# Graph attention: the masks of two chunks packed as the two bytes of one 16-bit number, and turned by one set of transposes

## The chip, the cores and the metric

One core of one Trainium2 chip. The metric is the device time of one execution in microseconds, as the median of several runs. The engines are TensorE (PE; PEld for its weight loads), VectorE (DVE), ScalarE (ACT), GpSimd (POOL) and SyncE (SP, which only issues transfers here). Each works through its own list of instructions in order, and they wait for one another by semaphores.

## The reference

For each of 8 graphs with 2048 nodes and 256 features (`x` is 8 x 2048 x 256 fp32, `adj` 8 x 2048 x 2048 int32, about one entry in 512 set):

```python
h  = relu(layernorm(x))
Wh = h @ W
f1, f2 = Wh @ a[:256], Wh @ a[256:]
e  = leaky_relu(f1[:, None] + f2[None, :], 0.2)
p  = softmax(where(adj > 0, e, -9e15), axis=0)   # over i: each column j sums to one
out = x + elu(p @ Wh)
```

The softmax runs down the columns of `adj`. The kernel therefore keeps column j on a partition and the 2048 rows i along the free dimension, and needs the mask in that turned layout.

## The kernel before, in words

A batch is one graph. Its 2048 columns are taken as 16 chunks of 128 (128 chunks in all, CH). The main loop has a step s per chunk; every engine runs the same list of steps, written out in its own order, and works on chunks at different distances from s.

- **Masks.** GpSimd issues `load_raw(pair)` (L880 to L883) every second step: 1 MB of `adj`, 2048 rows by 256 columns, turned from int32 into bf16 by the transfer, into one of two buffers `raw`. VectorE makes one mask per step, `make_mask(s + 2)` (L762): 0 where there is an edge and -2^56 where there is none, as bf16, from one half of the columns. TensorE turns it in 16 transposes of 128 x 128 bf16 into `tp`, two banks of PSUM (L434 to L440), one chunk per step: `transpose_mask(s + 1)`, after the block of stored products and before the transposes of x.
- **Scores.** VectorE adds the turned mask to `f1_row` (f1 of all rows i, on every partition) and takes the maximum in the same instruction, into `prob` (L773). TensorE may turn the next mask only when these scores are read (`wait(pe, scores, c)`), as there is one `tp`.
- **Softmax.** ScalarE adds f2, applies the leaky ReLU (L590), negates the maximum (L592) and takes the exponential with its sum (L598). GpSimd makes the inverse of the sum (L890, L893) and the high fp16 half of the first 1024 probabilities (`direct`, L896); ScalarE makes the high half of the other 1024 (`stored`, L604); VectorE makes both low halves (L787, L792).
- **Products.** TensorE multiplies the direct halves with Wh in the next step (L504, L506, L511: 24 matmuls), and one row block of the stored halves of eight chunks (L486 to L488: 24 matmuls). Finished row blocks are scaled, given the ELU and added to x (L620 to L651, L806, L812, L916).
- **Projections, 17 chunks ahead.** x comes in chunks of 128 rows (`load_x`, L346), VectorE takes the statistics (L737, L742), GpSimd normalises (L910), TensorE transposes and multiplies with W (L429, L417). f1 is written to memory and read back onto all partitions (`f1_row`). For the last quarter of a batch that is a round trip just before the next batch's first scores.

The order of VectorE in a step is: scores(s), statistics, mask(s + 2), low half of Wh(s + 17), low halves of chunk s - 1, then what finishes a row block. The order of GpSimd is: inverse and product of chunk s - 1, normalise, an addition by transfer (L916), the load of a mask pair.

The lines that the change turns on:

```python
nc.vector.tensor_scalar(neg[:, c % 2], raw[:, pair % 2, :, c % 2 * P:(c % 2 + 1) * P], 0.0, -NOT_AN_EDGE, ALU.is_le, ALU.mult)
...
for m in range(C):
    last = nc.tensor.transpose(tp_b[:, m * P:(m + 1) * P], neg[:, c % 2, m, :], ident_b[:])
```

Of the kernel before, what the change touches and what calls it, by code (L numbers as in the profile page):

```python
# [6 lines left out]
ALU = mybir.AluOpType  # L7
# [2 lines left out]
F32 = mybir.dt.float32  # L10
F16 = mybir.dt.float16
BF16 = mybir.dt.bfloat16

P = 128
ALPHA = 0.2
EPS = 1e-5
NOT_AN_EDGE = 2.0 ** 56
P_BITS = 14
W_TOP = 16.0


def graph_attention(nc, x, adj, W, a, out):

    B, N, F = x.shape
# [23 lines left out]
    with ExitStack() as ctx:  # L50
# [6 lines left out]
        def sem(name):  # L57
            return ctx.enter_context(nc.semaphore(name))

        raw = sb("raw", [P, 2, C, 2 * P], BF16)  # L60
        neg = sb("neg", [P, 2, C, P], BF16)
        f1_row = sb("f1_row", [P, 2, N], F32)
        prob = sb("prob", [P, 2, N + 2], F32)
        direct = sb("direct", [P, 2, 2, HALF], F16)
# [38 lines left out]
        tp = psum("tp", [P, 2, 512], F32)  # L103
        pre = psum("pre", [P, 512], F32)
        tp_b = tp[:].rearrange("p h c -> p (h c)").bitcast(BF16)
        acc_banks = acc[:].rearrange("p (h m) o -> p h (m o)", m=2)

        raw_in = [sem(f"raw_in{i}") for i in range(2)]
        x_in_s = [sem(f"x_in_s{i}") for i in range(RX)]
        x_early_in = [sem(f"x_early_in{i}") for i in range(4 + EARLY // 4 - 1)]  # L110
        x_res_in = [sem(f"x_res_in{i}") for i in range(RY)]
# [206 lines left out]
        def rows_of(tensor, k):  # L318
            b, i = finishing[k]
            if single(k):  # L320
                r = (2 * NB - 2 + (i == 8)) * P
                return tensor[b, r:r + P, :].rearrange("(t p) f -> p t f", p=P)
            r = (NB + 2 * i if i < 4 else 2 * (i - 4)) * P
            return tensor[b, r:r + 2 * P, :].rearrange("(t p) f -> p t f", p=P)

        def h_prime(k):
            b, i = finishing[k]
# [8 lines left out]
        def y_buf(k):  # L336
            return y[:, k % RY, 0:width(k) // FO, :]

        finish_index = {item: k for k, item in enumerate(finishing)}

        block = ctx.enter_context(nc.Block())

        @block.sync
        def _(sp):
            def load_x(c):
                if c - RX >= EARLY:  # L346
                    sp.wait_ge(xn_ready, c - RX + 1)
                sp.dma_start(x_buf(c), x[c // C, c % C * P:(c % C + 1) * P, :]).then_inc(x_in_s[(c - EARLY) % RX], 16)

            def write_f1(piece):  # L350
                index = pieces_sent(piece)
                sp.wait_ge(f1_turned, index + 1)
                b, q = divmod(piece, 4)
                rows = f1_dram[b, 512 * q:512 * (q + 1)].rearrange("(c g r) -> g c r", g=4, r=32)
                for g in range(4):
                    sp.dma_start(rows[g], f1_t[32 * g:32 * g + 4, index % 2, :]).then_inc(f1_written[index % 2], 16)

            def read_f1(piece):
                index = pieces_sent(piece)
                b, q = divmod(piece, 4)  # L360
                sp.wait_ge(f1_written[index % 2], 64 * (index // 2 + 1))
                wait(sp, scores, C * (b - 1))
                sp.dma_start(f1_row[:, b % 2, 512 * q:512 * (q + 1)],
                             f1_dram[b:b + 1, 512 * q:512 * (q + 1)].to_broadcast([P, 512])
                             ).then_inc(f1_row_in[b % 2], 16)

            def load_y(step):
                for k in finish(step):
                    wait(sp, y_out[k % RY], 16 * (k // RY))
                    sp.dma_start(y_buf(k), rows_of(x, k)).then_inc(x_res_in[k % RY], 16)  # L370

            def send_y(step):
                for k in finish(step):
                    wait_for_y(sp, k)
                    sp.dma_start(rows_of(out, k), y_buf(k)).then_inc(y_out[k % RY], 16)

            for c in range(4):
                sp.dma_start(x_buf(c), x[0, c * P:(c + 1) * P, :]).then_inc(x_early_in[c], 16)
                if c == 0:
                    sp.dma_start(w_raw, W.rearrange("(k p) o -> p k o", p=P)).then_inc(w_in, 16)  # L380
                    sp.dma_start(a_one, a.rearrange("o one -> one o")).then_inc(a_in, 16)
            for g in range(1, EARLY // 4):
                r = 4 * g % C * P
                sp.dma_start(x_early[:, 4 * g:4 * g + 4, :],
                             x[4 * g // C, r:r + 4 * P, :].rearrange("(c p) f -> p c f", p=P)
                             ).then_inc(x_early_in[3 + g], 16)
            for c in range(EARLY, EARLY + RX):
                load_x(c)
            for s in range(FIRST, END + 2):
                if chunk(s + 24) and s + 24 >= EARLY + RX:  # L390
                    load_x(s + 24)
                if chunk(s + LEAD - 1) and (s + LEAD - 1) % 4 == 3 and read_alone((s + LEAD - 1) // 4):
                    read_f1((s + LEAD - 1) // 4)
                if s <= CH + 2:
                    load_y(s + 1)
                    send_y(s - 2)
                else:
                    send_y(s - 1)
                    load_y(s + 1)
                if chunk(s + LEAD) and (s + LEAD) % 4 == 3 and sent((s + LEAD) // 4):  # L400
                    write_f1((s + LEAD) // 4)
                    if (s + LEAD) // 4 % 4 > 0:
                        read_f1((s + LEAD) // 4 - 1)
            for i in range(RY):
                sp.wait_ge(y_out[i], 16 * len([k for k in range(len(finishing)) if k % RY == i]))

        @block.tensor
        def _(pe):
# [21 lines left out]
                                               ident[:])  # L430
                last.then_inc(xt_ready, 1)

            def transpose_mask(c):
                pe.wait_ge(neg_ready, c + 1)  # L434
                if c == 0:
                    pe.wait_ge(ident_ready, 1)
                wait(pe, scores, c)
                for m in range(C):
                    last = nc.tensor.transpose(tp_b[:, m * P:(m + 1) * P], neg[:, c % 2, m, :], ident_b[:])  # L439
                last.then_inc(tp_ready, 1)  # L440

            def warm_up(count):
# [98 lines left out]
            for s in range(-18, 0):  # L541
                if s == -1:
                    spread_last_f1()
                    transpose_mask(0)
                transpose_x(s + LEAD + 1)
                if chunk(s + LEAD):
                    make_wh(s + LEAD)
            for s in range(END + 2):
# [4 lines left out]
                    extra_blocks(s - 2)  # L553
                if n is not None:
                    store_block(n)
                if chunk(s + 1):
                    transpose_mask(s + 1)
                if chunk(s + LEAD + 1):
                    transpose_x(s + LEAD + 1)
                if chunk(s - 1):  # L560
# [131 lines left out]
        def _(dve):  # L692
# [12 lines left out]
            def multiply_w(i):  # L705
                k, side = divmod(i, 2)
                dve.wait_ge(a_spread, 1)
                nc.vector.tensor_tensor_reduce(
                    out=w_a[:, i, :], in0=w_raw[:, k, :], in1=a_row[:, side, :], scale=1.0, scalar=0.0,
                    op0=ALU.mult, op1=ALU.add, accum_out=w_cat[:, k, FO + side:FO + side + 1]).then_inc(w_ready, 1)  # L710

            def largest_of_all():
# [42 lines left out]
                nc.vector.scalar_tensor_tensor(out=offset[:, rs], in0=mv[:, rs, 0], scalar=-1.0, in1=rstd[:, rs],  # L755
                                               op0=ALU.mult, op1=ALU.mult).then_inc(offset_s, 1)

            def make_mask(c):
                pair = c // 2
                dve.wait_ge(raw_in[pair % 2], 16 * (pair // 2 + 1))  # L760
                wait(dve, tp_ready, c - 1)
                nc.vector.tensor_scalar(neg[:, c % 2], raw[:, pair % 2, :, c % 2 * P:(c % 2 + 1) * P], 0.0, -NOT_AN_EDGE, ALU.is_le, ALU.mult  # L762
                                        ).then_inc(neg_ready, 1)

            def mask_scores(c):
                b, j = divmod(c, C)
                dve.wait_ge(tp_ready, c + 1)
                if j == 0:
                    dve.wait_ge(f1_row_in[b % 2], 64 * (b // 2 + 1) - (16 if b % 2 == 0 else 0))
                if c == 0:  # L770
                    dve.wait_ge(f1_last, 1)
                wait(dve, lo_stored, c - 1)
                nc.vector.tensor_tensor_reduce(  # L773
                    out=prob[:, c % 2, 0:N], in0=tp_b, in1=f1_row[:, b % 2, :], scale=1.0, scalar=-3.0e38,
                    op0=ALU.add, op1=ALU.max, accum_out=prob[:, c % 2, N:N + 1]).then_inc(scores, 1)

            def split_v_low(c):
                dve.wait_ge(v_hi, c + 1)
# [41 lines left out]
            for s in range(FIRST, END + 2):  # L820
# [20 lines left out]
                    multiply_w(3)  # L841
                if offset_at(s) is not None and s >= 0:
                    make_offset(offset_at(s))
                if chunk(s + 2) and s >= 0:
                    make_mask(s + 2)
                if s == 0:
                    split_v_low(LEAD - 1)
                if chunk(s + LEAD) and s != -1:
# [2 lines left out]
                    turn_f1((s + LEAD) // 4)  # L851
                if chunk(s - 1):
                    split_low(s - 1)
                if s == -5:
                    make_mask(0)
                if s == -4:
                    make_mask(1)
                for k in finish(s - 1 if s <= CH + 1 else s):
                    finish_elu(k)
                n = block_at(s)  # L860
# [4 lines left out]
        def _(pool):  # L865
# [10 lines left out]
            pool.wait_ge(const_ready, 1)  # L876


            def load_raw(pair):
                wait(pool, neg_ready, 2 * pair - 2)  # L880
                b, q = divmod(pair, C // 2)
                nc.gpsimd.dma_start(raw[:, pair % 2], adj[b].rearrange("(c p) j -> p c j", p=P)[  # L882
                    :, :, 2 * P * q:2 * P * (q + 1)]).then_inc(raw_in[pair % 2], 16)  # L883

            def split_high(c):
                p = prob[:, c % 2, :]
# [32 lines left out]
            for s in range(FIRST, END + 2):  # L919
# [4 lines left out]
                for k in finish(s - 2):  # L924
                    if k < summed_by_dma:
                        finish_add(k)
                if s % 2 == 0 and s >= 0 and chunk(s + 4):
                    load_raw(s // 2 + 2)
                if s == -22:
                    normalise(0)  # L930
                if 0 < s + LEAD + 2 and s < 0:
                    normalise(s + LEAD + 2)
                if s == -16:
                    load_raw(0)
                if s == -12:
                    load_raw(1)
                if s == -24:
                    root(0)
                if s == -21:
# [21 lines left out]
```

## Time and profile before

| | us |
|---|---|
| median of 3 runs | 992.19 (990.35 to 992.49) |
| the profiled execution | 987.88 |
| its span | 986.1 |
| PE busy | 950.0 |
| DVE busy | 920.7 |
| ACT busy | 879.3 |
| POOL busy | 645.3 |

The span runs from the first to the last instruction of the profiled execution; its time has 1.8 us more around it. Busy times are unions over the span and include time in which an instruction has started but is held up. Matmuls overlap in the pipeline, so the mean duration of one (0.27 us) is longer than the distance to the next (0.11 us).

### The profile page before, as it was taken

How to read it: one execution, taken by the hardware profiler on the slowest of the kernel's cores; microseconds unless marked ns; L12 is line 12 of the kernel's file. 1: busy time of each engine (PE TensorE's matmuls, PEld its weight loads, DVE VectorE, ACT ScalarE, POOL GpSimd, SP SyncE). 2: the span in 40 equal slices, each digit the busy share in tenths (PEclk: the TensorE clock that was granted, in tenths of full speed). 3: DMA queues.
4: the chain of work that ended last, by engine and by line, in shares of the span. 5: the costliest groups of instructions: out<-in, count | busy, mean ns of one | idle time of the engine just before them, and what ended most of it. 6: DMA issues, size and time to landing. Idle time of an engine off the chain costs nothing.

```text
span 986.1 us, 23861 instructions
## 1 busy us (share of the span) xinstructions
PE 950.0 (96%) x8993; PEld 840.0 (85%) x8993; DVE 920.7 (93%) x1271; ACT 879.3 (89%) x1237; POOL 645.3 (65%) x676
## 2 busy tenths in 40 slices
PE   8878999999999999999999999999999999999996
PEld 6666888889888898888888888888988989898896
DVE  8799989999899998999989998999999999999975
ACT  4788989999999999999999899999999999898985
POOL 6567665776766776876767776677676775555540
PEclk8899999999999999999999999999999999999898
DMA  9477667889879889799979988979987978979724
GB/s 233 83 107 108 97 108 122 147 162 156 149 136 176 146 155 167 119 180 149 161 147 144 173 148 151 154 141 172 156 163 123 172 133 138 170 113 158 143 65 140
DMA packets 199093, 142.13 MB, mean 144 GB/s; under 512 B 7361, under 2 KB 187841, under 8 KB 198978
## 3 DMA queue, kind: packets, MB, share of 16 engines
q0 software_dynamic: 140160, 81.80, 61.5%
q1 hardware_dynamic: 58818, 58.81, 20.8%
q8 instruction: 72, 1.18, 0.5%
q14 instruction: 43, 0.35, 0.1%
HBM read 176.16 MB, written 16.84 MB: 196 GB/s over the span
## 4 chain that ended last, share of the span: by engine, by line
POOL 32%; PE 30%; issue 25%; DVE 5%; DMA 4%; ACT 2%; POOLq 0%; SPq 0%; DVEq 0%; ACTq 0%
POOL direct L896 10%; POOL xn L910 6%; POOL raw L882 5%; POOL inv L893 4%; PE acc L511 4%; PE acc L504 4%; PE acc L506 4%; PE tp L439 3%; PE acc_st L486 3%; PE acc_st L487 3%; PE acc_st L488 3%; POOL y L916 3%; PE pre L417 3%; POOL rstd L904 2%; POOL small_total L890 2%
## 5 line engine op out<-in xcount | busy, mean ns | idle before, releaser
L773 DVE CUSTOM_DVE_ANT_0 prob<-tp,f_row 128x2048 f32<-128x2048 bf16 x128 | 292.0, 2282 | 21.5 <-DMA f_row<-f_scratch 14.9
L590 ACT ACTIVATE prob<-prob,f 128x2049 f32<-128x2049 f32 x128 | 257.6, 2013 | 5.4 <-DVE prob L773 5.4
L486 PE MATMUL acc_st<-v,stored 128*128 128x256 f16 x960 | 261.5, 272 | 0.8 <-ACT part L620 0.8
L488 PE MATMUL acc_st<-v,stored 128*128 128x256 f16 x960 | 261.7, 273 | 0.0
L487 PE MATMUL acc_st<-v,stored 128*128 128x256 f16 x960 | 261.6, 273 | 0.0
L598 ACT ACTIVATE prob<-prob,shift 128x2048 f32<-128x2048 f32 x128 | 256.5, 2004 | 4.0
L896 POOL TENSOR_TENSOR direct<-prob,inv 128x1024 f16<-128x1024 f32 x128 | 243.5, 1902 | 10.0
L504 PE MATMUL acc<-v,direct 128*128 128x256 f16 x1024 | 233.4, 275 | 5.4 <-ACT z_direct L626 3.5
L506 PE MATMUL acc<-v,direct 128*128 128x256 f16 x1024 | 233.3, 274 | 0.0
L890 POOL TENSOR_SCALAR small_total<-total 128x1 f32<-128x1 f32 x128 | 29.8, 233 | 272.8 <-ACT prob L598 271.4
L604 ACT ACTIVATE stored<-prob,inv 128x1024 f16<-128x1024 f32 x128 | 146.1, 1142 | 47.6 <-POOL inv L893 47.6
L787 DVE SCALAR_TENSOR_TENSOR direct<-prob,inv,direct 128x1024 f16<-128x1024 f32 x128 | 162.0, 1266 | 12.2 <-POOL direct L896 12.1
L792 DVE SCALAR_TENSOR_TENSOR stored<-prob,inv,stored 128x1024 f16<-128x1024 f32 x128 | 163.7, 1279 | 0.1
L439 PE MATMUL tp<-ident_b,neg 128*128 128x128 bf16 x2048 | 136.1, 220 | 6.1 <-DVE prob L773 6.1
L439 PEld LDWEIGHTS tp<-ident_b,neg 128*128 128x128 bf16 x2048 | 125.4, 98 | 12.1 <-issue 9.2
L511 PE MATMUL acc<-v,direct 128*128 128x256 f16 x1024 | 133.6, 274 | 0.0
L762 DVE TENSOR_SCALAR neg<-raw 128x2048 bf16<-128x2048 bf16 x128 | 129.9, 1015 | 0.8 <-DMA raw<-in_adj 0.8
L417 PE MATMUL pre<-w_cat,h_t 128*128 128x258 f32 x444 | 117.8, 388 | 4.6 <-ACT h_t L610 4.1
L504 PEld LDWEIGHTS acc<-v,direct 128*128 128x128 f16 x1024 | 100.9, 99 | 17.7 <-ACT z_direct L626 4.9
L487 PEld LDWEIGHTS acc_st<-v,stored 128*128 128x128 f16 x960 | 93.7, 98 | 22.0
L506 PEld LDWEIGHTS acc<-v,direct 128*128 128x128 f16 x1024 | 100.9, 99 | 12.0
L910 POOL TENSOR_SCALAR xn<-x_in,rstd,offset 128x256 f32<-128x256 f32 x108 | 107.3, 994 | 5.4 <-DVE offset L755 3.0
(94 smaller groups left out, 1383.9 us busy)
## 6 DMA issues: line engine op xcount, KB each, us to landing
raw<-in_adj POOLq DMA_DIRECT2D x64, 1024.0 KB, 11.2
y<-in_x SPq DMA_DIRECT2D x63, 256.0 KB, 3.1
out<-y SPq DMA_DIRECT2D x63, 256.0 KB, 2.2
y<-elu POOLq DMA_DIRECT2D x56, 256.0 KB, 5.0
x_in<-in_x SPq DMA_DIRECT2D x108, 128.0 KB, 3.3
f_row<-f_scratch SPq DMA_DIRECT2D x31, 256.0 KB, 6.5
stored<-in_x SPq DMA_DIRECT2D x4, 512.0 KB, 6.9
f_scratch<-f_t SPq DMA_DIRECT2D x124, 0.5 KB
```

Of the source, the lines that this page charges most:

```text
L439: last = nc.tensor.transpose(tp_b[:, m * P:(m + 1) * P], neg[:, c % 2, m, :], ident_b[:])
L486: nc.tensor.matmul(bank[:, 0:FO], p_st[:, 0, rows], v_c[:, 0, :], start=(c == 0), stop=False)
L487: nc.tensor.matmul(bank[:, 0:FO], p_st[:, 0, rows], v_c[:, 1, :], start=False, stop=False)
L488: last = nc.tensor.matmul(bank[:, 0:FO], p_st[:, 1, rows], v_c[:, 0, :], start=False, stop=(c == G - 1))
L504: nc.tensor.matmul(acc[:, m, :], p_d[:, 0, rows], v_c[:, 0, :], start=(j == 0 and m % 2 == 0), stop=False, skip_group_check=True)
L506: nc.tensor.matmul(acc[:, m, :], p_d[:, 0, rows], v_c[:, 1, :], start=False, stop=False, skip_group_check=True)
L511: last = nc.tensor.matmul(acc[:, m, :], p_d[:, 1, rows], v_c[:, 0, :], start=False, stop=(j == C - 1), skip_group_check=True)
L590: nc.scalar.activation(p_top, p_top, ACT.Prelu, bias=f2, alpha=ALPHA).then_inc(leaky, 1)
L598: nc.scalar.activation(p, p, ACT.Exp, bias=shift[:, c % R:c % R + 1], accum_out=total[:, c % R:c % R + 1]).then_inc(prob_ready, 1)
L773: nc.vector.tensor_tensor_reduce(out=prob[:, c % 2, 0:N], in0=tp_b, in1=f1_row[:, b % 2, :], scale=1.0, scalar=-3.0e38, op0=ALU.add, op1=A ...
L896: nc.gpsimd.tensor_tensor(direct[:, c % 2, 0, :], p[:, 0:HALF], k.to_broadcast([P, HALF]), ALU.mult).then_inc(hi_direct, 1)
L910: nc.gpsimd.tensor_scalar(xn_buf(c), x_buf(c), rstd[:, c % RS:c % RS + 1], offset[:, c % RS:c % RS + 1], ALU.mult, ALU.add).then_inc(xn_re ...
```

## The change

The mask becomes one byte: 0 for an edge, 192 for none. Columns 2k and 2k + 1 of a 256-column stretch of `adj` go to two different chunks (even columns to the one, odd ones to the other), so that the bytes of neighbouring columns form one 16-bit number. 16 transposes of these numbers, as bf16, turn both chunks at once, every second step; the scores instruction reads every second byte of `tp`. It subtracts f1, scaled by 2^-48 in advance, from the byte and multiplies by -2^48, which gives f1 where there is an edge and f1 - 192 x 2^48 elsewhere.

As chunks are now alternate columns, rows of x, of the output and the order of i follow: chunk 2q + t holds rows 256q + 2p + t. A mask instruction takes the even or the odd rows i of a 256-column stretch and makes half of both chunks' masks; it still has 2048 elements. The loads are halved in size and doubled in number (four buffers of half the size). Masks are made one step earlier (s + 3 in place of s + 2), and a pair's transposes come on odd steps.

```diff
 BF16 = mybir.dt.bfloat16
+U8 = mybir.dt.uint8
 P = 128
...
 EPS = 1e-5
-NOT_AN_EDGE = 2.0 ** 56
+F1_SCALE = 2.0 ** -48
+NOT_AN_EDGE = 192.0
 P_BITS = 14
...
             return ctx.enter_context(nc.semaphore(name))
-        raw = sb("raw", [P, 2, C, 2 * P], BF16)
+        raw = sb("raw", [P, 4, G, 2 * P], BF16)
         neg = sb("neg", [P, 2, C, P], BF16)
+        neg_bytes = neg[:].rearrange("p b m j -> p b (m j)").bitcast(U8).rearrange("p b (t q j) -> p b t q j", t=2, q=G)
         f1_row = sb("f1_row", [P, 2, N], F32)
...
         tp_b = tp[:].rearrange("p h c -> p (h c)").bitcast(BF16)
+        tp_bytes = tp[:].rearrange("p h c -> p (h c)").bitcast(U8).rearrange("p (i t) -> p t i", t=2)
         acc_banks = acc[:].rearrange("p (h m) o -> p h (m o)", m=2)
-        raw_in = [sem(f"raw_in{i}") for i in range(2)]
+        raw_in = [sem(f"raw_in{i}") for i in range(4)]
         x_in_s = [sem(f"x_in_s{i}") for i in range(RX)]
...
             if single(k):
-                r = (2 * NB - 2 + (i == 8)) * P
-                return tensor[b, r:r + P, :].rearrange("(t p) f -> p t f", p=P)
+                r = (2 * NB - 2) * P
+                return tensor[b, r:r + 2 * P, :].rearrange("(p t) f -> p t f", p=P)[:, (i == 8):(i == 8) + 1, :]
             r = (NB + 2 * i if i < 4 else 2 * (i - 4)) * P
-            return tensor[b, r:r + 2 * P, :].rearrange("(t p) f -> p t f", p=P)
+            return tensor[b, r:r + 2 * P, :].rearrange("(p t) f -> p t f", p=P)
         def h_prime(k):
...
             return y[:, k % RY, 0:width(k) // FO, :]
+        def x_rows(c):
+            b, j = divmod(c, C)
+            q, t = divmod(j, 2)
+            return x[b, 2 * P * q:2 * P * (q + 1), :].rearrange("(p t) f -> t p f", t=2)[t]
+        def masks_at(s):
+            if s < 0:
+                return [s + 5] if s >= -5 and s < -3 else []
+            return [2, 3] if s == 0 else ([s + 3] if s + 3 < CH else [])
         finish_index = {item: k for k, item in enumerate(finishing)}
...
                     sp.wait_ge(xn_ready, c - RX + 1)
-                sp.dma_start(x_buf(c), x[c // C, c % C * P:(c % C + 1) * P, :]).then_inc(x_in_s[(c - EARLY) % RX], 16)
+                sp.dma_start(x_buf(c), x_rows(c)).then_inc(x_in_s[(c - EARLY) % RX], 16)
             def write_f1(piece):
...
             for c in range(4):
-                sp.dma_start(x_buf(c), x[0, c * P:(c + 1) * P, :]).then_inc(x_early_in[c], 16)
+                sp.dma_start(x_buf(c), x_rows(c)).then_inc(x_early_in[c], 16)
                 if c == 0:
...
                 r = 4 * g % C * P
-                sp.dma_start(x_early[:, 4 * g:4 * g + 4, :],
-                             x[4 * g // C, r:r + 4 * P, :].rearrange("(c p) f -> p c f", p=P)
+                sp.dma_start(x_early[:, 4 * g:4 * g + 4, :].rearrange("p (q t) f -> p q (t f)", t=2),
+                             x[4 * g // C, r:r + 4 * P, :].rearrange("(q p t) f -> p q (t f)", p=P, t=2)
                              ).then_inc(x_early_in[3 + g], 16)
...
                 last.then_inc(xt_ready, 1)
-            def transpose_mask(c):
-                pe.wait_ge(neg_ready, c + 1)
-                if c == 0:
+            def transpose_masks(pair):
+                pe.wait_ge(neg_ready, 2 * pair + 2)
+                if pair == 0:
                     pe.wait_ge(ident_ready, 1)
-                wait(pe, scores, c)
+                wait(pe, scores, 2 * pair)
                 for m in range(C):
-                    last = nc.tensor.transpose(tp_b[:, m * P:(m + 1) * P], neg[:, c % 2, m, :], ident_b[:])
+                    last = nc.tensor.transpose(tp_b[:, m * P:(m + 1) * P], neg[:, pair % 2, m % 2 * G + m // 2, :],
+                                               ident_b[:])
                 last.then_inc(tp_ready, 1)
...
                     spread_last_f1()
-                    transpose_mask(0)
+                    transpose_masks(0)
                 transpose_x(s + LEAD + 1)
...
                     store_block(n)
-                if chunk(s + 1):
-                    transpose_mask(s + 1)
+                if chunk(s + 1) and s % 2 == 1:
+                    transpose_masks((s + 1) // 2)
                 if chunk(s + LEAD + 1):
...
                 nc.vector.tensor_tensor_reduce(
-                    out=w_a[:, i, :], in0=w_raw[:, k, :], in1=a_row[:, side, :], scale=1.0, scalar=0.0,
+                    out=w_a[:, i, :], in0=w_raw[:, k, :], in1=a_row[:, side, :], scale=(F1_SCALE, 1.0)[side], scalar=0.0,
                     op0=ALU.mult, op1=ALU.add, accum_out=w_cat[:, k, FO + side:FO + side + 1]).then_inc(w_ready, 1)
...
                                                op0=ALU.mult, op1=ALU.mult).then_inc(offset_s, 1)
-            def make_mask(c):
-                pair = c // 2
-                dve.wait_ge(raw_in[pair % 2], 16 * (pair // 2 + 1))
-                wait(dve, tp_ready, c - 1)
-                nc.vector.tensor_scalar(neg[:, c % 2], raw[:, pair % 2, :, c % 2 * P:(c % 2 + 1) * P], 0.0, -NOT_AN_EDGE, ALU.is_le, ALU.mult
-                                        ).then_inc(neg_ready, 1)
+            def make_masks(n):
+                pair, t = divmod(n, 2)
+                dve.wait_ge(raw_in[n % 4], 16 * (n // 4 + 1))
+                wait(dve, tp_ready, pair - 1)
+                nc.vector.tensor_scalar(neg_bytes[:, pair % 2, t], raw[:, n % 4], 0.0, NOT_AN_EDGE,
+                                        ALU.is_le, ALU.mult).then_inc(neg_ready, 1)
             def mask_scores(c):
                 b, j = divmod(c, C)
-                dve.wait_ge(tp_ready, c + 1)
+                dve.wait_ge(tp_ready, c // 2 + 1)
                 if j == 0:
...
                 nc.vector.tensor_tensor_reduce(
-                    out=prob[:, c % 2, 0:N], in0=tp_b, in1=f1_row[:, b % 2, :], scale=1.0, scalar=-3.0e38,
-                    op0=ALU.add, op1=ALU.max, accum_out=prob[:, c % 2, N:N + 1]).then_inc(scores, 1)
+                    out=prob[:, c % 2, 0:N], in0=tp_bytes[:, c % 2, :], in1=f1_row[:, b % 2, :], scale=-1.0 / F1_SCALE,
+                    scalar=-3.0e38, op0=ALU.subtract, op1=ALU.max, accum_out=prob[:, c % 2, N:N + 1]).then_inc(scores, 1)
             def split_v_low(c):
...
                     make_offset(offset_at(s))
-                if chunk(s + 2) and s >= 0:
-                    make_mask(s + 2)
+                for n in masks_at(s):
+                    make_masks(n)
                 if s == 0:
...
                     split_low(s - 1)
-                if s == -5:
-                    make_mask(0)
-                if s == -4:
-                    make_mask(1)
                 for k in finish(s - 1 if s <= CH + 1 else s):
...
             pool.wait_ge(const_ready, 1)
-            def load_raw(pair):
-                wait(pool, neg_ready, 2 * pair - 2)
+            def load_raw(n):
+                pair, t = divmod(n, 2)
+                wait(pool, neg_ready, n - 3)
                 b, q = divmod(pair, C // 2)
-                nc.gpsimd.dma_start(raw[:, pair % 2], adj[b].rearrange("(c p) j -> p c j", p=P)[
-                    :, :, 2 * P * q:2 * P * (q + 1)]).then_inc(raw_in[pair % 2], 16)
+                nc.gpsimd.dma_start(raw[:, n % 4], adj[b].rearrange("(q p t) j -> t p q j", p=P, t=2)[
+                    t, :, :, 2 * P * q:2 * P * (q + 1)]).then_inc(raw_in[n % 4], 16)
             def split_high(c):
...
                         finish_add(k)
-                if s % 2 == 0 and s >= 0 and chunk(s + 4):
-                    load_raw(s // 2 + 2)
+                if s >= -1 and chunk(s + 5):
+                    load_raw(s + 5)
                 if s == -22:
...
                     normalise(s + LEAD + 2)
-                if s == -16:
-                    load_raw(0)
-                if s == -12:
-                    load_raw(1)
+                if s in (-16, -15, -12, -11):
+                    load_raw((-16, -15, -12, -11).index(s))
                 if s == -24:
```

## Rows read from the trace of the kernel before

**Rows 1.** Page, part 1: busy us (share of the span) x instructions of each engine.

```profile
span 986.1 us, 23861 instructions
PE 950.0 (96%) x8993; PEld 840.0 (85%) x8993; DVE 920.7 (93%) x1271; ACT 879.3 (89%) x1237; POOL 645.3 (65%) x676
```

**Rows 2.** Windows, by batch: us of each engine (x instructions), clock, DMA, GB/s.

```profile
core 0: us, PE busy (x) PEld busy (x) DVE busy (x) ACT busy (x) POOL busy (x), PEclk, DMA share, GB/s
32.10:144.60 112.50, 97.85 (x884) 82.75 (x883) 105.30 (x140) 98.17 (x138) 74.71 (x76) 0.97 0.68 102
144.60:730.30 585.70, 580.88 (x5597) 517.93 (x5596) 563.05 (x780) 544.32 (x769) 410.32 (x419) 1.00 0.88 152
730.30:846.00 115.70, 115.41 (x1121) 103.23 (x1120) 112.16 (x140) 108.15 (x151) 78.73 (x81) 1.00 0.87 148
846.00:949.00 103.00, 97.53 (x982) 86.86 (x980) 95.62 (x92) 92.44 (x98) 56.11 (x59) 0.97 0.77 129
949.00:986.10 37.10, 29.61 (x272) 26.30 (x269) 20.64 (x30) 21.22 (x32) 5.37 (x6) 0.93 0.38 122
```

**Rows 3.** Chain of waits, 400 to 420 us: start, us, engine, tile, line.

```profile
by line: PE pre L417 13.1%; PE acc_st L487 13.1%; PE acc_st L486 13.1%; PE acc L511 13.1%; PE acc_st L488 13.1%; PE acc L506 12.0%; PE acc L504 11.4%; PE tp L439 8.9%; PE pre L429 2.3%
...
405.55 0.89 PE tp L439 x16
...
412.79 0.89 PE tp L439 x16
```

**Rows 4.** Waits, 144.6 to 730.3 us: total us, times, longest.

```profile
POOL small_total L890 <- ACT prob L598: 155.6, 71, 4.6
ACT stored L604 <- POOL inv L893: 24.8, 41, 1.0
DVE prob L773 <- DMA f_row<-f_scratch: 13.7, 6, 3.0
ACT f L579 <- PE pre L417: 6.0, 24, 0.4
ACT prob L590 <- DVE prob L773: 4.1, 5, 1.4
```

**Rows 5.** Source view, VectorE lines: count, ns min/median/max, first and last start.

```profile
L762 DVE TENSOR_SCALAR neg<-raw x128: 675/715/2374, 27.3 to 938.3; 128x2048 bf16<-128x2048 bf16 x128
L773 DVE CUSTOM_DVE_ANT_0 prob<-tp,f_row x128: 2269/2278/2293, 32.1 to 949.0; 128x2048 f32<-128x2048 bf16 x128
L792 DVE SCALAR_TENSOR_TENSOR stored<-prob,inv,stored x128: 1270/1273/1419, 43.5 to 960.4; 128x1024 f16<-128x1024 f32 x128
```

**Rows 6.** Windows, by batch, of the mask instruction's line alone.

```profile
32.10:144.60 112.50, 15.37 (x16) 0.97 0.68 102
144.60:730.30 585.70, 74.70 (x80) 1.00 0.88 152
730.30:846.00 115.70, 19.69 (x16) 1.00 0.87 148
846.00:949.00 103.00, 18.51 (x14) 0.97 0.77 129
```

**Rows 7.** Timeline of VectorE, 424 to 426 us: start, us, line, tiles.

```profile
424.69 0.18 DVE L742 BATCH_NORM_AGGREGATE mv<-stats 128x2 f32<-128x6 f32 x1
424.79 0.89 DVE L762 TENSOR_SCALAR neg<-raw 128x2048 bf16<-128x2048 bf16 x1
425.61 0.41 DVE L779 TENSOR_TENSOR v<-pre,v 128x256 f16<-128x256 f32 x1
```

**Rows 8.** Timeline of GpSimd, 422 to 427 us.

```profile
423.25 1.90 POOL L896 TENSOR_TENSOR direct<-prob,inv 128x1024 f16<-128x1024 f32 x1
425.13 0.99 POOL L910 TENSOR_SCALAR xn<-x_in,rstd,offset 128x256 f32<-128x256 f32 x1
```

**Rows 9.** Page, part 6 (DMA issues), and the costliest lines: GpSimd's issues.

```profile
raw<-in_adj POOLq DMA_DIRECT2D x64, 1024.0 KB, 11.2
x_in<-in_x SPq DMA_DIRECT2D x108, 128.0 KB, 3.3
...
L882 POOL DMA_DIRECT2D raw<-in_adj x64 | 83.5, 1305 | 0.0
L916 POOL DMA_DIRECT2D y<-elu x56 | 52.1, 930 | 0.0
```

## The prediction

> **What bounds the kernel now.** I read the page's busy shares first [rows 1]: TensorE, VectorE and ScalarE are all near or above 90% busy, so no single share names the bound, and the next view has to be taken by stage. There are 128 chunks in eight batches of 16. Batches 1 to 5 are alike and take 585.7 us together (117.1 each), with TensorE busy for 580.9, VectorE for 563.1 and ScalarE for 544.3 [rows 2]. Batches 0, 6 and 7 have lighter VectorE work or an interrupted TensorE; 37 us of tail follow, and 32 us of head stand before.
>
> TensorE really is full. The chain of waits over one stretch of batch 3 is TensorE alone, and two successive bursts of mask transposes start 7.24 us apart, each 0.89 us long [rows 3]. So 16 transposes cost 0.89 us of a step, and 12% of TensorE's step is the thing that the change halves. But the other engines stand right behind it. VectorE lacks only 585.7 - 563.1 = 22.6 us over five batches, and 13.7 us of that are waits for f1's row at the batch edges [rows 4], which no faster TensorE shortens. ScalarE's 544.3 us become 579.2 with what it waits for the inverse (24.8), for TensorE's projections (6.0) and for scores (4.1) [rows 4]; the inverse is a reply that its own loop needs. So a shorter TensorE step uncovers engines that are only a few per cent shorter, and any VectorE time that the change adds is uncovered almost at once.
>
> **The change part by part.**
>
> *Transposes.* Sixteen per two chunks in place of 32: 64 bursts of 0.89 us less, 57 us of TensorE. In steps 1 to 126 the remaining bursts fall on odd steps, where they wait for the odd chunk's scores as each burst waits for its predecessor's now; the even chunk's scores come a step later, and the odd chunk's need no new transpose. Nothing is delayed by that.
>
> *The mask instruction.* Still one per chunk, still 2048 elements, but it writes bytes in place of 16-bit numbers. This is the term that decides. Its row now is 675 ns at least and 715 in the median [rows 5]. The score instruction on the same engine, with the same 2048 elements and two operands, takes 2278 ns [rows 5]. If both have the same fixed part, then one unit of work q solves a + q = 675 and a + 4q = 2278: q is 534 ns and a is 141 ns, so the mask runs four elements in the time in which the scores run one. No row shows a one-operand VectorE instruction of this size with a byte result. The two ends are therefore +0 (it stays at 675) and +1.60 us (it falls to 2278). The mask differs from every slow row in two ways, one tensor operand and 16-bit numbers on both sides, and the change takes the second away and leaves the first. I take the step between, two elements at a time: a + 2q = 1.21 us, +0.534 us per mask, which in ratio is also about as far from the one row as from the other. Both ends stay in the range or the rivals.
>
> The Trainium skill speaks to this place, and against the change: "DVE: opcode table, instruction layouts, handler registers and perf-mode slots", section 7, says that the engine's four-per-cycle mode is chosen only where source and destination are both 2 bytes wide, and that a one-source operation with a stream of another width is left with the one- and the two-per-cycle modes. "VectorE: DVE Perf Modes", in its tier table, gives 693 ns for 2048 bf16 elements and 1227 ns for 2048 fp32 elements of a one-source operation. The trace's 675 to 715 ns agree with the first; no run here shows the second, by which the term would be +0.53 us, as in the sum.
>
> *Its stalls.* The mask's mean is far above its minimum: 74.7 us for 80 masks, 20.7 more than 80 x 0.675 [rows 6]. What it waits for is GpSimd: a mask that starts at 424.79, while the product of 423.25 to 425.15 runs, takes 0.89 us, that is 0.36 until the product ends and then about the 0.53 of its pure work; the GpSimd instruction behind it (xn at 425.13) is stretched in its turn [rows 7, 8]. If VectorE becomes the slow engine, the product of the chunk before is ready earlier within VectorE's step, so I keep a quarter of these stalls (5 us over five batches) and both ends, 0 and 20.7.
>
> *Scores.* Same instruction and element count; its mask operand is read as every second byte of PSUM in place of every 16-bit number, with another constant. No row shows such a read. It writes one fp32 per 1.04 ns already, so I take no change; were it half as fast it would cost 2 us a step, and that is in the slow rival.
>
> *Loads of the mask.* 128 of half the size in place of 64. One issue holds GpSimd for 1.31 us now, and that of a 256 KB transfer for 0.93 [rows 9], so a half-size issue lies between 0.65 (half) and 1.31; at 1.1 GpSimd's 410.3 us over five batches become about 446 of 585.7 [rows 2]. What hides it is GpSimd's wait for the exponential, 155.6 us there [rows 4]. The lead is two steps, some 14.5 us, as before, against 11.2 us to landing for 1 MB now [rows 9]; without that cover the mask would wait for the load. Rows of x, of the residual and of the output are taken in pairs of the same 1 KB runs or longer ones; 3.3 us to landing for an x chunk [rows 9] has many steps of lead: nothing.
>
> **The sum.** Batches 1 to 5: VectorE without its stalls 563.1 - 20.7 = 542.4; 80 longer masks +42.7; the idle time of now, 22.6, which is mostly the batch edge's f1 row; a quarter of the stalls, 5. That is 612.7 against 585.7: +27.0. Batch 0 [rows 2, 6]: 105.3 - 4.6 + 8.5 = 109.2 on VectorE in 112.5; its 7.2 us of idle take up most of it: +2. Batch 6: 112.2 - 8.9 + 8.5 = 111.8, with 3.5 idle and 1 of stalls 116.3 against 115.7: +0.6. Batch 7 (14 masks): 95.6 - 9.1 + 7.5 = 94.0, with its 7.4 idle and 1 of stalls 102.4 against 103.0, and TensorE is freed: -1. Head: two masks before the first scores, +1. Tail: 0. In all +29.6. The profiled execution took 987.9 us (span 986.1 and 1.8 around it), so it would take 1017.5; the median of the runs lies 4.3 higher, which gives 1021.8. I put the forecast at 1019.
>
> The likeliest case's own range: down to 995 if all stalls vanish, half the idle time goes too, and batch 7 gains most of TensorE's 6 us; up to 1046 if all stalls stay and batch 0 pays in full.
>
> **Rivals.**
>
> *The mask keeps its rate* (or most of it), and the change is faster. Then TensorE's step falls to 6.8 us, and VectorE and ScalarE decide. ScalarE needs 579 us of 586 with its waits, so batches 1 to 5 gain 0 to 20 us; I take 10, with 2 in batch 6 and 3 in batch 7: 15 us, about 975. For it: 57 us of the fullest engine go, and nothing in the trace shows a byte result. Against it: the quick rate is seen only with 16-bit numbers on both sides.
>
> *The longer mask is swallowed.* VectorE's 20.7 us of stalls and 22.6 of idle over five batches (43.3) happen to equal the added 42.7. If all of it gives way, the batches stay at 117 us: 988 to 994, no change. Against it: the f1 row's wait is a round trip through memory at the batch edge that a longer mask doesn't shorten.
>
> *One element at a time.* The byte result (or the byte read in the scores) brings VectorE to the rate of the scores row: +1.60 us per mask. Batches 1 to 5: 542.4 + 128.2 + 22.6 + 5 = 698.2, +112; batch 0 +18, batch 6 +17, batch 7 +10, head +3: +160, about 1150. This decides from any price above the 0.28 us per mask that 22.6 us of VectorE idle over 80 masks can hide. For it: the other large VectorE rows run so, as the 1024 elements of the low half in 1273 ns [rows 5]. Against it: the mask keeps its single operand in SBUF.
>
> The side on which it ends hangs on the same point in all of them: below about 0.28 us per mask the saved transposes win or nothing is seen; above it VectorE sets a longer step.
>
> **Chances.** Half rate with VectorE as the bound 0.68; mask at its rate 0.15; swallowed 0.05; one at a time 0.12. A change of under 0.2% can't be told from none here. Faster: the second case and a little of the first's lower end, 0.16. Same: the swallowed case and a little beside it, 0.06. Slower: 0.78. The range, 976 to 1046, holds the likeliest case, the swallowed one and half of the faster one; it leaves out the one-at-a-time case and the other half of the faster, 0.2 together.
>
> **What would show it.** The mask's minimum should read 1.2 us (675 and 2278 are the rivals'), the scores 2.28. TensorE's bursts of mask transposes should be half as many, and TensorE should show gaps before the transposes or the direct products, its share falling to about 88% (893 of 1016 us). VectorE should have next to no idle in mid-batch, with steps of 7.6 us. GpSimd's wait for the exponential should stay above 1 us a step and no mask should wait for its load. The forecast is wrong if VectorE shows idle in mid-batch, if a mask waits for a transfer, or if a batch in the middle takes less than 117 us.

## The result, and the profile after

The changed kernel takes 1006.57 us (median of 4 runs, 1005.56 to 1007.15) against 992.34: ratio 1.0144, 95% interval 1.0125 to 1.0163. It is 14 us slower; the forecast was 1019. The profiled execution took 1005.56 us, 17.7 more than that of before (987.88, which lies further below its median).

The busy shares and the windows by batch of the changed kernel, with the columns of [rows 1] and [rows 2] (same batches, read at its own first scores):

```profile
span 1003.7 us, 21811 instructions
PE 918.0 (91%) x7969; PEld 782.7 (78%) x7969; DVE 960.0 (96%) x1271; ACT 879.8 (88%) x1237; POOL 752.7 (75%) x740
```

```profile
33.60:151.30 117.70, 96.67 (x751) 79.33 (x750) 113.13 (x141) 98.26 (x137) 84.88 (x82) 0.88 0.69 98
151.30:745.40 594.10, 558.86 (x4965) 482.02 (x4963) 585.61 (x779) 543.76 (x770) 482.00 (x461) 1.00 0.90 150
745.40:863.30 117.90, 110.69 (x989) 95.37 (x987) 116.80 (x140) 107.76 (x151) 91.29 (x87) 1.00 0.88 144
863.30:967.40 104.10, 92.10 (x863) 77.12 (x862) 99.24 (x90) 93.47 (x99) 65.57 (x65) 1.00 0.79 127
967.40:1003.70 36.30, 28.85 (x262) 25.16 (x259) 20.66 (x30) 21.29 (x32) 5.36 (x6) 0.96 0.36 125
```

VectorE is busy for 585.6 of the 594.1 us of batches 1 to 5; TensorE has dropped behind it. The chain of waits in mid-kernel (420 to 450 us), all TensorE before [rows 3], is now VectorE and pieces without a named wait ("issue"):

```profile
by line: issue 33.4%; DVE prob L792 23.4%; DVE stored L811 15.9%; DVE direct L806 15.8%; DVE v L798 5.5%; DVE z_st L825 5.1%; DVE stats L756 4.7%; DVE mv L761 1.0%; DVE neg L781 0.9%; DVEq L821 0.7%; DVEq L246 0.5%; DVE elu L831 0.4%; DVE f
```

The mask and scores of the changed kernel (source view, ns min/median/max, to be read against [rows 5]), and the mask's windows in batches 1 to 5 (against [rows 6]):

```profile
L781 DVE TENSOR_SCALAR neg<-raw x128: 1208/1224/2668, 27.8 to 950.5; 128x2048 uint8<-128x2048 bf16 x128
L792 DVE CUSTOM_DVE_ANT_0 prob<-tp,f_row x128: 2272/2280/2294, 33.6 to 967.4; 128x2048 f32<-128x2048 uint8 x128
```

```profile
151.30:745.40 594.10, 107.92 (x80) 1.00 0.90 150
```

The mask went from 675 to 1208 ns at least; the scores read every second byte at no price. VectorE's waits in batches 1 to 5 were 13.7 us for f1's row [rows 4]; now they are

```profile
DVE prob L792 <- DMA f_row<-f_scratch: 2.1, 3, 1.2
DVE prob L792 <- DVE stored L811: 0.3, 2, 0.2
```

### The profile page after: what moved, and what is told of

It is laid out like the page before. It is cut to its first block, busy times and chain, and to the rows that moved or that the text cites. A ratio compares the mean times of both kernels' runs of the same rounds, so it can differ in the third digit from the quotient of the medians.

```text
span 1003.7 us, 21811 instructions
## 1 busy us (share of the span) xinstructions
PE 918.0 (91%) x7969; PEld 782.7 (78%) x7969; DVE 960.0 (96%) x1271; ACT 879.8 (88%) x1237; POOL 752.7 (75%) x740
## 4 chain that ended last, share of the span: by engine, by line
DVE 46%; issue 32%; POOL 10%; DMA 5%; PE 4%; ACT 2%; DVEq 1%; SPq 1%; POOLq 0%; ACTq 0%
DVE stored L811 11%; DVE direct L806 11%; DVE prob L792 10%; DVE v L798 4%; POOL direct L912 4%; DVE stats L756 3%; DVE neg L781 3%; DMA f_row<-f_scratch 2%; DMA f_scratch<-f_t 2%; POOL raw L898 2%; DVE z_st L825 1%; POOL inv L909 1%; POOL y L932 1%; DVE elu L831 1%; DVE mv L761 1%
## 5 line engine op out<-in xcount | busy, mean ns | idle before, releaser
L792 DVE CUSTOM_DVE_ANT_0 prob<-tp,f_row 128x2048 f32<-128x2048 uint8 x128 | 292.2, 2283 | 10.0 <-DMA f_row<-f_scratch 4.4
L523 PE MATMUL acc<-v,direct 128*128 128x256 f16 x1024 | 236.9, 277 | 8.7 <-ACT z_direct L645 5.0
L525 PE MATMUL acc<-v,direct 128*128 128x256 f16 x1024 | 236.6, 277 | 0.0
L781 DVE TENSOR_SCALAR neg<-raw 128x2048 uint8<-128x2048 bf16 x128 | 182.0, 1423 | 0.0
L906 POOL TENSOR_SCALAR small_total<-total 128x1 f32<-128x1 f32 x128 | 41.1, 321 | 179.8 <-ACT prob L617 136.3
L898 POOL DMA_DIRECT2D raw<-in_adj x128 | 156.3, 1221 | 0.2 <-POOL xn L926 0.2
L530 PE MATMUL acc<-v,direct 128*128 128x256 f16 x1024 | 134.5, 275 | 1.6 <-DVE direct L806 1.6
L926 POOL TENSOR_SCALAR xn<-x_in,rstd,offset 128x256 f32<-128x256 f32 x108 | 123.1, 1140 | 12.2 <-DVE offset L774 12.1
L523 PEld LDWEIGHTS acc<-v,direct 128*128 128x128 f16 x1024 | 101.9, 100 | 23.2 <-ACT z_direct L645 7.0
L530 PEld LDWEIGHTS acc<-v,direct 128*128 128x128 f16 x1024 | 100.4, 99 | 15.8 <-DVE direct L806 3.5
L525 PEld LDWEIGHTS acc<-v,direct 128*128 128x128 f16 x1024 | 101.7, 99 | 13.0
```

The source lines that it names most:

```text
L523: nc.tensor.matmul(acc[:, m, :], p_d[:, 0, rows], v_c[:, 0, :], start=(j == 0 and m % 2 == 0), stop=False, skip_group_check=True)
L525: nc.tensor.matmul(acc[:, m, :], p_d[:, 0, rows], v_c[:, 1, :], start=False, stop=False, skip_group_check=True)
L530: last = nc.tensor.matmul(acc[:, m, :], p_d[:, 1, rows], v_c[:, 0, :], start=False, stop=(j == C - 1), skip_group_check=True)
L792: nc.vector.tensor_tensor_reduce(out=prob[:, c % 2, 0:N], in0=tp_bytes[:, c % 2, :], in1=f1_row[:, b % 2, :], scale=-1.0 / F1_SCALE, scala ...
```

## The experiments

Theory A: the byte result halves the mask's rate, VectorE becomes the bound, and the halved transposes are worth nothing at that price. The rivals: the doubled loads on GpSimd (B), TensorE still sharing the bound (C). Ratios are against the kernel before.

**The mask at its old rate (e1).** The changed kernel with 16-bit results (not the masks of the graph):

```diff
-                nc.vector.tensor_scalar(neg_bytes[:, pair % 2, t], raw[:, n % 4], 0.0, NOT_AN_EDGE,
-                                        ALU.is_le, ALU.mult).then_inc(neg_ready, 1)
+                out16 = neg[:, pair % 2].rearrange("p (q t) j -> p q (t j)", t=2) if t else raw[:, n % 4]
+                nc.vector.tensor_scalar(out16, raw[:, n % 4], 0.0, -6.0234375, ALU.is_le, ALU.mult).then_inc(neg_ready, 1)
```

> The changed kernel, but each mask instruction writes 2048 16-bit numbers (the even one over its own input, the odd one over both halves of the mask buffer), so the masks are not those of the graph; transposes, loads and waits stay. Theory A (the loss is VectorE's time for the byte result): the mask is back at 0.68 us at least, VectorE falls by about 0.52 us a mask, and with TensorE at 16 transposes per two chunks the time falls below the kernel before, to 965 to 982, with ScalarE as the next bound. Theory B (the loss comes from the doubled issues on GpSimd or from TensorE's idle time and lower clock in batch 0): it stays above 998.

Measured 975.2 us, ratio 0.9803 (0.9757 to 0.9849). Its mask rows and its batches 1 to 5:

```profile
L782 DVE TENSOR_SCALAR raw<-raw x64: 675/686/1978, 27.9 to 914.1; 128x2048 bf16<-128x2048 bf16 x64
L782 DVE TENSOR_SCALAR neg<-raw x64: 675/706/2258, 28.8 to 920.6; 128x2048 bf16<-128x2048 bf16 x64
```

```profile
147.40:721.90 574.50, 556.40 (x4966) 482.22 (x4965) 558.07 (x780) 541.16 (x771) 434.88 (x459) 1.00 0.93 155
```

Of the mask only the width, the value and the place of the result differ, and 31 us go. The doubled loads are still there, so they aren't the loss; the other edits together gain 17 us on the kernel before. That ScalarE would be the next bound isn't shown: it is busy for 541 of the 574.5 us, TensorE for 556 and VectorE for 558. Batch 0, 5.2 us longer in the changed kernel, is back at its old length here, though TensorE's granted clock there is 0.89 as against 0.88 in the changed kernel and 0.97 before:

```profile
34.80:147.40 112.60, 92.67 (x740) 76.82 (x739) 107.21 (x141) 96.81 (x133) 75.51 (x80) 0.89 0.72 102
```

**The transposes doubled again (e2).** In the changed kernel, `for m in [*range(C), *range(C)]` in place of `for m in range(C)`.

> The changed kernel with each pair's 16 transposes done twice, so that TensorE has as many as before (0.89 us more on every odd step). Theory A (VectorE alone sets the step now): TensorE's step of 7.23 us still fits under VectorE's 7.43, 1004 to 1012. Rival C (TensorE still shares the bound and its relief won part of what the mask lost): up to 57 us more, at least 1020.

Measured 1007.9 us, ratio 1.0146 (1.0105 to 1.0187), beside 1.0144 with one set. Batches 1 to 5:

```profile
152.20:750.90 598.70, 586.29 (x5608) 517.51 (x5606) 586.37 (x779) 545.58 (x771) 480.93 (x461) 1.00 0.87 149
```

TensorE is as busy as VectorE again, and the median doesn't show it (this profile is of the longest of four executions, 1011.3 us). At the byte result's price the halved transposes bought nothing beyond the 4 us or so that the intervals leave open. C falls.

**Half-size loads alone,** in the kernel before: one half per step (e3), then both halves in the even step (e5, whose edit is shown):

```diff
-                dve.wait_ge(raw_in[pair % 2], 16 * (pair // 2 + 1))
+                dve.wait_ge(raw_in[pair % 2], 32 * (pair // 2 + 1))
...
                 if s % 2 == 0 and s >= 0 and chunk(s + 4):
-                    load_raw(s // 2 + 2)
+                    load_raw(s + 4)
+                    load_raw(s + 5)
```

> The kernel before with its mask loads cut into two of half the size, one issued per step; nothing else changed. Theory A: GpSimd has the room, 990 to 995, GpSimd's busy time up by some 70 us. Theory B (the doubled issues are what costs): at least 8 us more, 1000 or above.

> The kernel before with its mask loads cut into two of half the size, both issued in the even step, so that the second has the same lead as the whole one had (in the first try of this kind it had one step less, and the masks waited 106 us for loads). Theory A: GpSimd has the room for the doubled issues, 984 to 995, and if the wait of the first scores of a batch for f1's row comes from being read behind a 1 MB load, that wait falls from 14.9 us to under 8. Theory B (the doubled issues cost by themselves): 1000 or above.

One half per step: 1037.1 us, ratio 1.0431 (1.0393 to 1.0469). The number is B's, the cause isn't. A chunk of this kernel needs both halves, so the second had one step of lead in place of two, and the masks waited:

```profile
DVE neg L762 <- DMA raw<-in_adj: 105.9, 51, 4.1
```

The run was badly designed for B. With both in time: 989.4 us, ratio 0.9971 (0.9950 to 0.9992). The wait for f1's row over the whole span, in the kernel before and in this one, and the issues of this one:

```profile
DVE prob L773 <- DMA f_row<-f_scratch: 14.9, 7, 3.0
```

```profile
DVE prob L773 <- DMA f_row<-f_scratch: 10.9, 6, 2.5
```

```profile
L883 POOL DMA_DIRECT2D raw<-in_adj x128 | 124.1, 990 | 0.0
```

GpSimd has the room, so B falls. The wait for f1's row is 10.9 us in place of 14.9, not under 8: the size of the loads explains a part of it at most. These are single executions, and in the next experiment the kernel with whole loads shows 18.3.

**How much VectorE can swallow.** One more instruction per step, in the kernel before (e6) and in the changed one (e7):

```diff
+                if chunk(s):
+                    nc.vector.bn_stats(idle_stats[:, s % 2, :], f1_row[:, s // C % 2, 0:256])
```

> The kernel before with one more VectorE instruction per step behind the mask, statistics of 256 elements of f1's row that nobody reads: 0.45 us from start to start, 58 us in all. Theory A (VectorE had stalls and waits that give way when it is asked for more): some 40 of the 58 vanish, 1002 to 1015. Rival C (in the changed kernel it was TensorE's relief that took up the most of the added mask time, and here TensorE has none): 1025 or above.

> The changed kernel with the same extra VectorE instruction per step, 0.45 us each, 58 us in all. Theory A (VectorE sets the step now and has 1 to 2 us a batch left of its slack): nearly all of it is seen, 1052 to 1066. Rival (as much gives way as in the change itself): 1035 or less.

Both expectations mis-sized the dose. From the instruction's start to that of the next is 0.34 us in this place (423.23 to 423.57 below, in the kernel before with it), not the 0.45 that it takes where the next instruction waits for its result: 43 us in all, 27 in batches 1 to 5.

```profile
423.23 0.42 DVE L848 BATCH_NORM_STATS2 idle_stats<-f_row 128x6 f32<-128x256 f32 x1
423.57 0.41 DVE L780 TENSOR_TENSOR v<-pre,v 128x256 f16<-128x256 f32 x1
```

The kernel before: 994.6 us, ratio 1.0030 (1.0008 to 1.0052), 3 us more than 991.1. The changed kernel: 1036.1, ratio 1.0453 (1.0425 to 1.0481), 29 more than 1006.6. Batches 1 to 5 of the two, before first:

```profile
145.60:738.60 593.00, 585.26 (x5623) 520.68 (x5621) 572.73 (x860) 545.07 (x773) 406.83 (x422) 1.00 0.87 150
```

```profile
155.30:772.40 617.10, 559.68 (x4963) 482.25 (x4961) 609.49 (x860) 545.68 (x769) 480.57 (x460) 1.00 0.86 144
```

Of 27 us the kernel before shows 7.3 there and the changed one 23. That is a knee: VectorE had about 0.25 us a step to give, without any relief of TensorE, and the change has used it up. (The two profiled executions of the kernel before, with and without the instruction, lie 9.3 us apart and the medians only 3, so the 7.3 is rather too much and the 0.25 too little.) Outside these batches the changed kernel still swallows more than half: some 7 of 16 us show. Both times miss the expected bands of theory A, 994.6 below 1002 to 1015 and 1036.1 below 1052 to 1066; the second misses its rival's by 1 us too. With a dose of 43 in place of 58, the 40 us that theory A let vanish in the kernel before did; "nearly all of it is seen" holds for batches 1 to 5 of the changed kernel, not for the whole, where 29 of 43 show.

**Both bytes at once (e4).** The transfer makes bytes, and one 16-bit operation turns two of them over; this needs `adj` to be 0 or 1, as the inputs are.

```diff
-        raw = sb("raw", [P, 4, G, 2 * P], BF16)
+        raw = sb("raw", [P, 4, G, 2 * P], U8)
+        raw_pairs = raw[:].rearrange("p b q j -> p b (q j)").bitcast(U16)
...
+        neg_pairs = neg[:].rearrange("p b m j -> p b (m j)").bitcast(U16).rearrange("p b (t i) -> p b t i", t=2)
...
-                nc.vector.tensor_scalar(neg_bytes[:, pair % 2, t], raw[:, n % 4], 0.0, NOT_AN_EDGE,
-                                        ALU.is_le, ALU.mult).then_inc(neg_ready, 1)
+                nc.vector.tensor_scalar(neg_pairs[:, pair % 2, t], raw_pairs[:, n % 4], 257.0, -NOT_AN_EDGE,
+                                        ALU.subtract, ALU.mult).then_inc(neg_ready, 1)
```

> The changed kernel, but the transfer turns the int32 entries into bytes (0 or 1, as the inputs are), and VectorE takes two neighbouring bytes as one unsigned 16-bit number n and writes (257 - n) x 192, which is both mask bytes at once: 1024 elements of 16 bits per mask in place of 2048 with a byte result. Theory A: at the rate of the mask before that is 0.14 + 0.27 = 0.41 us, 0.8 us less than now; VectorE is no longer the bound, ScalarE and TensorE are, 958 to 978. Rival D: the transfer writes pieces of 256 bytes in place of 512, and if it is paid by the piece and slower with small ones, the masks wait for their loads: above 1000, with idle time of VectorE in front of the mask.

Measured 968.8 us, ratio 0.9748 (0.9712 to 0.9785): faster than both kernels, by 23 and 38 us. Its mask, its loads, and batches 1 to 5:

```profile
L784 DVE TENSOR_SCALAR neg<-raw x128: 409/583/1986, 27.1 to 913.2; 128x1024 uint16<-128x1024 uint16 x128
```

```profile
raw<-in_adj POOLq DMA_DIRECT2D x128, 256.0 KB, 8.0
```

```profile
145.50:716.20 570.70, 555.26 (x4964) 482.16 (x4963) 552.79 (x779) 539.91 (x769) 412.54 (x459) 1.00 0.94 119
```

0.41 us at least, as expected, and no mask waits for its load. The transfers with 256-byte pieces land in 8.0 us, as the 512-byte ones did (7.9), though they write half the bytes. Both read the same int32 entries, so this doesn't tell a price by the piece from one by the bytes read; no wait comes of it, and rival D falls.

**The same with the transposes doubled (e8).**

> The kernel in which the transfer makes the bytes and the mask takes 0.41 us, with each pair's transposes done twice. Theory A (the halved transposes are worth something only where VectorE's mask is cheap): TensorE is the bound again at 7.23 us a step, 980 to 993, that is 11 to 24 above the same kernel with one set, while at the byte result's price the doubled set cost nothing that could be measured. Rival (ScalarE or VectorE set the step there whatever TensorE does): 967 to 973.

Measured 988.4 us, ratio 0.9967 (0.9951 to 0.9983). TensorE is the bound again:

```profile
150.90:734.40 583.50, 581.01 (x5603) 518.78 (x5602) 561.75 (x780) 543.95 (x769) 416.46 (x459) 1.00 0.89 117
```

So the second set of transposes costs 20 us where the mask is cheap, and 1 us, inside the intervals, where it writes bytes. The halved transposes are worth something only beside a cheap mask. The cheap mask is worth about 20 us even with the doubled transposes (988.4 against 1007.9), and 38 with the halved ones.

## Why the prediction was right in its direction, and too large

*The mask's price* was right: 1.209 us worked out at two elements at a time, 1.208 measured, and for 1024 elements at the mask's old rate the same two constants give 0.408, with 0.409 measured (e4). The Trainium skill ("DVE: opcode table, instruction layouts, handler registers and perf-mode slots", section 7) says that the four-per-cycle mode needs 2-byte numbers on both sides, and that a one-source operation with an fp8 or fp32 stream is left with the one- and the two-per-cycle modes. The trace agrees: the byte result lost half the rate (1208 ns), the 16-bit ones kept it (675 and 409 ns).

*VectorE as the bound* was right (e2, e6, e7 and the chain), and so was the faster rival's time: 975 was forecast for a mask at its old rate, 975.2 measured. That it fits to 0.2 us is luck: the profiled executions differ by 12.3 us and the medians by 17, where 15 were forecast.

*The size* was off in batches 1 to 5: +27.0 forecast, +8.4 measured. The sum added the longer masks to a VectorE that keeps its idle time, and that step failed in three terms:
- the idle time, kept at 22.6 us, is 8.5. By far the most of these 14 us is the wait for f1's row, which I held to be a fixed round trip: 13.7 us before, 2.1 after. VectorE's coming later explains a part of it at most. Over the whole span the wait is 4.4 us in the changed kernel, 2.9 with the extra instruction (e7), and still only 6.4 and 7.6 where the change's mask is short (e1, e4); in the kernel before it is 14.9, and 18.3 with the extra instruction (e6). So most of it went with the change's other edits. Half-size loads alone show 10.9 (e5); which of the edits does the rest is open.
- what I took as VectorE's own work held another 11 us that went: mostly the stalls of the small instructions that make the variance and the offset, 10.2 and 6.9 us in these batches before, 4.7 and 2.6 after. They are held up as the mask is. In one step of before, the variance's ends when GpSimd's product does (439.58); in one of after, the product has ended before it starts (at 422.37):

```profile
437.68 1.90 POOL L896 TENSOR_TENSOR direct<-prob,inv 128x1024 f16<-128x1024 f32 x1
```

```profile
438.79 0.80 DVE L749 TENSOR_SCALAR var_eps<-mv 128x4 f32<-128x4 f32 x1
```

```profile
422.84 0.17 DVE L768 TENSOR_SCALAR var_eps<-mv 128x4 f32<-128x4 f32 x1
```

- the other way, the mask's stalls are 107.9 - 80 x 1.208 = 11.3 us, not the 5 that I kept.

The three are -14, -11 and +6: the 18.6 us of the miss. The swallowed rival, at 0.05, named two of the reserves, the idle time and the mask's stalls, but not the small instructions; four fifths of the added 42.7 us did go unseen in these batches. The other stretches were under-sized, with +2.6 forecast and +9.2 measured (batch 0 +5.2, batch 6 +2.2, batch 7 +1.1, head +1.5, tail -0.8). Batch 0's 5 us come with the byte masks, of whose price I let all but 2 us vanish there: with 16-bit masks (e1) it takes 112.6 us, against 112.5 before. Batches 6 and 7 take 114.7 and 100.9 us in e1, less than before, so their excess comes with the byte masks too; the head's doesn't (34.8 us in e1), and its cause is open. TensorE's granted clock in batch 0, 0.88 against 0.97, isn't the cause, since it is 0.89 in e1.

The forecast of 1019 was put 3 us below its own sum, 1021.8, without a reason. Against the sum the median is 15 us lower: 18.6 too much in batches 1 to 5, 6.6 too little elsewhere, and 3.3 because the profiled execution of before lies 4.3 below the median and that of after only 1.0. So the errors partly cancel.

*Loads:* the price of an issue was forecast at 1.1 us and is 1.22, inside its bounds; no mask waits for a load. GpSimd's busy time in batches 1 to 5 is 482.0 us, though, not 446.

*The other signs:* VectorE's step is 7.43 us (594.1 / 80), not 7.6. GpSimd's wait for the exponential fell from 155.6 to 59.9 us in batches 1 to 5, that is 0.75 a step and not above 1; another 30.0 us of the same instruction's waits are now put down to VectorE. TensorE's share was 91%, not 88%: the time is shorter, and its busy time fell by 32 us and not by the 57 of the bursts. The mean matmul of the stored products lasts 273 ns in both kernels; where the other 25 us went was not found.

## What to carry to other kernels

Where several engines lie within a few per cent of each other, relief for the fullest is worth nothing once the price paid for it on the next exceeds what that one has to give, here about 0.25 us a step: price the trade on the engine that pays, element width first. A busy share holds two kinds of time, work and stalls, and the stalls give way first; so a term added to the second engine has to be set against its stalls, also those inside "busy" small instructions, before it is put on the time. If the packing is wanted, find the form that keeps 16-bit numbers on both sides.

## What the runs showed of the hardware that was not expected

The mask lengthens what GpSimd does beside it, and the longer mask more so. GpSimd's normalisation takes 0.55 us at least. Its median is 0.72 us with masks of 0.41 us (e4), 0.99 with masks of 0.68 (before) and 1.46 with masks of 1.21 (after); in the changed kernel 42 of the 108 take the 0.55 and the others 1.5 to 1.6. The three kernels in this order:

```profile
L929 POOL TENSOR_SCALAR xn<-x_in,rstd,offset x108: 548/719/1597, 45.6 to 805.6; 128x256 f32<-128x256 f32 x108
```

```profile
L910 POOL TENSOR_SCALAR xn<-x_in,rstd,offset x108: 553/989/1598, 42.3 to 820.0; 128x256 f32<-128x256 f32 x108
```

```profile
L926 POOL TENSOR_SCALAR xn<-x_in,rstd,offset x108: 548/1457/1626, 43.4 to 837.9; 128x256 f32<-128x256 f32 x108
```

With byte masks, issues of transfers are lengthened too. In the changed kernel, a mask from 422.93 to 424.16 and GpSimd's issue of the addition beside it, which takes 1.41 us against 0.93 of [rows 9]:

```profile
422.93 1.23 DVE L781 TENSOR_SCALAR neg<-raw 128x2048 uint8<-128x2048 bf16 x1
```

```profile
422.86 1.41 POOL L932 DMA_DIRECT2D y<-elu  x1
```

Of the 56 such issues the 22 that have a mask beside them for 0.5 us or more take 1.37 us in the mean, the other 34 0.95. With 16-bit masks none takes more than 0.98 (e1 and the kernel before).

An issue of a half-size load takes 0.99 us in the kernel before (e5), 1.09 in the changed one with 16-bit masks (e1), and 1.22 with byte masks; 1 MB in one took 1.31. Halving a load here leaves three quarters or more of the price of its issue.
